# The boundary rows two steps behind VectorE's part, and all three quarters scaled by ScalarE, in a graph network's gather loop

## The reference

```python
h = jnp.maximum(_layernorm(x, axis=-1), 0.0)
# layer 0: attention over the edges, 4 heads, 8 relations
feat_all = jnp.einsum('ni,rhid->rnhd', inputs, conv_weights)
e = jax.nn.leaky_relu(el + er, negative_slope=LEAKY_SLOPE)
ex = jnp.exp(e - m[edge_dst])                     # m: maximum over a destination's edges
alpha = ex / denom[edge_dst]
h = jax.ops.segment_sum(alpha[..., None] * feat_src_e, edge_dst, num_segments=N_NODES)
x = x + h + h_bias
h = jnp.maximum(_layernorm(x, axis=-1), 0.0)
# layer 1: three rounds of mean aggregation, of which the loop prepares the first
h = h @ W_in + b_in
agg = segment_sum(h[src], dst) / deg;  h = relu(agg @ W_agg[l] + h @ W_self[l] + b_hid[l])
```

## Time and profile before

| | us |
|---|---|
| median of 3 runs (2577.82 to 2600.36) | 2599.94 |
| profiled execution, its time | 2594.63 |
| profiled execution, its span | 2592.7 |
| edge loop: first scores (L1393) to last carried row (L1293) | 637.9 to 1461.7 |
| from there to the first load of the next phase | 65.2 |
| busy in the span: PE, DVE, ACT, POOL | 2173, 1388, 718, 585 |

### The profile page before, as it was taken

How to read it: one execution, slowest core, us unless ns; L and a number is a source line. 1 busy time by engine, 2 the same in 40 slices (tenths; PEclk the granted TensorE clock), 3 DMA queues, 4 the chain that set the end, 5 groups by cost and what they waited for, 6 DMA issues and landing times. The chain is left out here.

```text
span 2592.7 us, 29932 instructions
## 1 busy us (share of the span) xinstructions
PE 2173.1 (84%) x9258; PEld 1197.8 (46%) x9259; DVE 1387.6 (54%) x3828; ACT 718.1 (28%) x2133; POOL 584.9 (23%) x549
## 2 busy tenths in 40 slices
PE   2389999995777786778776749999989999999999
PEld 1243334333555464556554424444544444544445
DVE  5779999994456564555565528878821111101001
ACT  0134444442445453445444521010000001000000
POOL 3200000004776665757575100000000000000000
PEclk7589999997776787877777879999989999999999
DMA  5024444445444443535353323222222222233432
GB/s 148 15 97 147 154 148 154 157 154 173 125 126 129 124 140 99 150 103 156 109 152 109 69 89 102 92 82 82 71 83 90 82 86 87 82 115 98 124 98 81
DMA packets 249540, 290.31 MB, mean 112 GB/s; under 512 B 53330, under 2 KB 212247, under 8 KB 249111
## 3 DMA queue, kind: packets, MB, share of 16 engines
q1 hardware_dynamic: 195278, 181.12, 22.8%
q0 software_dynamic: 24192, 67.12, 9.9%
q10 hardware_dynamic: 29896, 39.99, 4.4%
HBM read 201.20 MB, written 86.96 MB: 111 GB/s over the span
## 5 line engine op out<-in xcount | busy, mean ns | idle before, releaser
L1905 PE MATMUL PS<-a_sb,y_sb 128*128 128x512 f16 (+2 forms) x4320 | 874.3, 363 | 43.5 <-DVE y_sb L1981 30.9
L1070 POOL DMA_INDIRECT work<-feat_tab,fidx_i x504 | 543.9, 1079 | 791.3 <-issue 653.1
L1905 PEld LDWEIGHTS PS<-a_sb,y_sb 128*128 128x128 bf16 (+1 forms) x4320 | 407.9, 98 | 509.7 <-issue 69.7
L1275 PE MATMUL PS<-work,stg 128*128 128x260 f32 x1008 | 328.4, 483 | 3.2 <-issue 2.4
L1130 ACT ACTIVATE work<-work 128x64 f32<-128x64 f32 x1344 | 327.3, 332 | 7.5 <-issue 7.1
L233 DVE TENSOR_SCALAR side<-iota_c,col_t 128x512 f16<-128x512 f16 x940 | 329.0, 350 | 0.2
L243 PE MATMUL PS<-side 128*128 128x512 f16 x940 | 254.2, 383 | 20.2 <-DVE side L233 12.4
L1275 PEld LDWEIGHTS PS<-work,stg 128*128 128x128 f32 x1008 | 231.7, 242 | 71.1 <-issue 24.6
L1995 DVE TENSOR_TENSOR mean<-PS,rdeg 128x1024 f32<-128x1024 f32 (+1 forms) x24 | 27.2, 1134 | 416.0 <-PE PS L1905 415.7
L1847 ACT ACTIVATE hT<-mean,bh_c 128x512 f32<-128x512 f32 (+1 forms) x48 | 30.3, 678 | 789.4 <-DVE mean L1999 789.4
L232 DVE TENSOR_SCALAR side<-iota_c,rel 128x128 f16<-128x128 f16 x940 | 236.4, 251 | 0.2 <-PE PS L243 0.2
(11 more groups left out here) (243 smaller groups left out, 1637.0 us busy)
## 6 DMA issues: line engine op xcount, KB each, us to landing
a_sb<-a_tab SPq DMA_DIRECT2D x126, 640.0 KB, 4.3
feat_tab<-stg ACTq DMA_DIRECT2D x120, 260.0 KB, 2.1
a_tab<-side SPq DMA_DIRECT2D x235, 128.0 KB, 1.7
stg<-dst_tab SPq DMA_DIRECT2D x42, 384.0 KB
work<-feat_tab,fidx_i POOLq DMA_INDIRECT x504
h_tab<-outs SPq DMA_DIRECT2D x42, 130.0 KB
h_tab<-outs SPq DMA_DIRECT2D x8, 520.0 KB, 3.2
stg<-h_tab SPq DMA_DIRECT2D x8, 520.0 KB
```

The lines of the kernel that those rows point to most:

```text
L1070: pool.indirect_dma_start(out=ring[:, s, 0:FE], out_offset=None, in_=feat_tab[:, :], in_offset=bass.IndirectOffsetOnAxis(ap=idx, axis=0)). ...
L1275: mm = pe.matmul(PS[:, OUTS[j], 0:EXT], onehot[:, t, :], ring[:, j * U + t, 0:EXT], start=(t == 0), stop=(t == U - 1), skip_group_check=True)
L1905: mm = pe.matmul(SUMS(ug, n)[:, f, :], y_sb[l % 2][0:rows_of, kb, s, f * P:(f + 1) * P], a_sb[0:rows_of, load % SLOTS, kb % KB, 0:n], star ...
```

## The change

- **Scaling.** ACT scales quarter 0 as well, right behind the exponential and ahead of `keep`; DVE's multiplication goes. PE's quarter 0 waits for ACT in place of DVE.
- **Boundary rows.** DVE's part (`ready`) and ACT's `root` stay where they were. PE's and ACT's rows of a chunk now come two steps later (`rows`, at `s - 3 in CHUNK_END`), for chunks 0 to 5.
- **The last two chunks.** Chunk 7 gets its own two PSUM banks and buffers, and the rows of chunks 6 and 7 are done in turns behind the loop (`tail`).
- The output copy goes to the buffer of the first bias copy, no longer to that of ReLU, so the wait for the previous store moves from `turned` to `inner`. SP's stores follow the new places.

```diff
@@ walk(eng, step, begin, ready, rows, tail)
                     step(s // G, s % G, last=(s == SUBS - 1))
                     if s - 1 in CHUNK_END:
-                        part(CHUNK_END.index(s - 1))
-                part(NC - 1)
-                part(NC)
+                        ready(CHUNK_END.index(s - 1))
+                    if s - 3 in CHUNK_END:
+                        rows(CHUNK_END.index(s - 3))
+                tail()
...
@@ ACT step
-                    for half in range(2):
-                        scale(i, j, 2, half)
+                    scale(i, j, 2)
...
                         act.wait_ge(s_rs, num(i, j, 2, 2))
                         weigh(*nxt)
+                        act.wait_ge(s_ex, num(*nxt, 1, 2))
+                        scale(*nxt, 0)
                     keep(i, j)
                     if not last:
-                        act.wait_ge(s_ex, num(*nxt, 1, 2))
-                        for half in range(2):
-                            scale(*nxt, 1, half)
+                        scale(*nxt, 1)
...
+                def tail():
+                    turned(LATE - 1)
+                    root(LATE)
+                    inner(LATE - 1)
+                    turned(LATE)
+                    outer(LATE - 1)
+                    inner(LATE)
+                    outer(LATE)
@@ PE quarter_sum
-                    if q:
-                        pe.wait_ge(s_sa, num(i, j, NQT - 1, q))
-                    else:
-                        pe.wait_ge(s_sd, num(i, j, 1, 1))
+                    pe.wait_ge(s_sa, num(i, j, NQT, q + 1))
...
+                def tail():
+                    turn(LATE - 1)
+                    inner(LATE - 1)
+                    turn(LATE)
+                    outer(LATE - 1)
+                    inner(LATE)
+                    outer(LATE)
@@ DVE
-                def scale(i, j):
-                    dve.wait_ge(s_ex, num(i, j, 1, 2))
-                    tiles = slice(j * U, j * U + QT)
-                    rows = ring[:, tiles, 0:F].rearrange("p u (h d) -> p u h d", h=H)
-                    dve.tensor_tensor(rows, rows, ring[:, tiles, F:FE].unsqueeze(3).to_broadcast([P, QT, H, D]), ALU.mult
-                                      ).then_inc(s_sd, 1)
...
                         bring(i, j)
-                    if not last:
-                        scale(*nxt)
```

More of the change, by code:

```diff
@@ L1039, in at, with walk @@
             return s // G, s % G
-        def walk(eng, step, part, begin):
+        def walk(eng, step, begin, ready, rows, tail):
             with when(eng, 3):
@@ L1058, in walk @@
                     chunk(eng, c, turn)
-                    part(c)
-                part(NC)
+                    if c < NC - 1:
+                        ready(c)
+                        if c:
+                            rows(c - 1)
+                tail()
         with nc.Block() as block:
@@ L1123, in weigh, with scale @@
                     act.activation(fac[:, 0:H], fac_x[:, 0:H], ACT.Exp).then_inc(s_fx, 1)
[L1125 to L1126 removed]
+                def scale(i, j, q):
+                    for u in range(QT):
                         s = j * U + q * QT + u
@@ L1169, in root, with inner, outer, rows @@
                     act.activation(std[:, 0, :], mv[:, 0, :, 1], ACT.Sqrt, bias=eps_c[:, :]).then_inc(s_sd2, 1)
-                def rest(c):
-                    act.wait_ge(s_wi, c + 1)
+                def inner(d):
+                    bank, to = BANKS[late(d)], k2(kept_in[late(d)])
+                    act.wait_ge(s_wi, d + 1)
+                    if d < LATE:
+                        act.wait_ge(s_st, 16 * d + 16)
                     for f in range(K2):
-                        act.activation(k2(h0)[:, f, :], BOUND[:, f, :], ACT.Identity, bias=bin_c[:, f:f + 1]
-                                       ).then_inc(s_h0, 1)
+                        act.activation(to[:, f, :], bank[:, f, :], ACT.Identity, bias=bin_c[:, f:f + 1]).then_inc(s_h0, 1)
                     for f in range(K2):
-                        act.activation(hT[:, f, c * CW:(c + 1) * CW], BOUND[:, f, :], ACT.Identity,
+                        act.activation(hT[:, f, d * CW:(d + 1) * CW], bank[:, f, :], ACT.Identity,
                                        bias=bin_c[:, f:f + 1]).then_inc(s_h0, 1)
[L1179 to L1189, removed]
+                def outer(d):
+                    act.wait_ge(s_t3, d + 1)
+                    act.activation(kept_in[late(d)].rearrange("p (j n) -> p j n", j=2), BANKS[late(d)], ACT.Copy
+                                   ).then_inc(s_tb, 1)
+                def rows(d):
+                    turned(d)
+                    inner(d)
+                    outer(d)
+                def tail():
[6 more added lines that the diff above has]
+                    outer(LATE)
                 def begin(dynamic):
@@ L1196, in begin @@
                     act.wait_ge(s_ex, 2)
-                    for half in range(2):
-                        scale(0, 0, 1, half)
-                walk(act, step, part, begin)
+                    scale(0, 0, 0)
+                    scale(0, 0, 1)
+                walk(act, step, begin, root, rows, tail)
             @block.tensor
@@ L1336, in _ @@
                 pe.wait_ge(built.evicted, NREAL)
-                walk(pe, step, part, begin)
+                walk(pe, step, begin, lambda c: None, rows, tail)
             @block.vector
@@ L1496, in part @@
                     ln_stats(dve, rows, c, 0, s_bs, s_vr)
-                    wait_past(dve, s_t2, c)
-                    ln_finish(dve, rows, c, 0, s_sd2, s_rs2, s_hn, hn)
+                    if c < LATE:
+                        wait_past(dve, s_t2, c)
+                    ln_finish(dve, rows, c, 0, s_sd2, s_rs2, s_hn, hn[late(c)])
                     dve.wait_ge(s_hn, 4 * c + 4)
@@ L1514, in begin @@
                     onehots(0, 0, 1)
-                    scale(0, 0)
-                walk(dve, step, part, begin)
+                walk(dve, step, begin, ready, lambda d: None, lambda: ready(LATE))
             @block.sync
```

82 lines of the change are left out of this document (44 added, 38 removed).

## The result

| | before | after |
|---|---|---|
| median of 4 runs each, us | 2599.06 | 2665.88 |
| ratio, 95% interval | | 1.028 (1.022 to 1.034) |
| profiled execution, span | 2592.7 | 2666.8 |
| first gather to first score | 28.4 | 53.0 |
| first to last score of the loop | 802.1 | 864.9 |

The change makes the kernel 67 us slower; the forecast was 2608, no difference that can be told. A second profile of each kernel gave 30.6, 796.3 (before) and 52.4, 853.9 (after) for the middle two rows.

The account below looks back on a forecast made before the run. The prediction took the chain between PE, DVE and ACT, not gathers, to bound the loop. Scaling +6, boundary +25 and behind the loop -18 gave +13 on 2594.6: 2608 us, 8 in 10 from 2565 to 2650.

Parts of the forecast that it names:

- Scaling, +6: Edge loop steps: moving quarter 0's scaling from DVE to ACT adds 6 us in sum, bounds -34 to +49.
- steps of 18 us have room for it: Plain loop steps: the common 18.0 us step absorbs ACT's added scaling, since its chain needs at least 15.3 us.
- its sign: Profile after, plain stretches of the loop: 18.0 to 18.5 us a step expected.
- seven short steps at 2.4 us: Loop steps under 15 us: each takes at least 2.4 us more through ACT's longer chain, 17 us for seven.
- The ring is full and gathers do not pace the loop: Edge loop: POOL's gathers wait for PE's quarter sums, 110.8 us; the chain between PE, DVE and ACT paces it.
- Boundary, +25: Chunk boundaries in the loop: DVE's parts and rows done apart cost 92 us instead of 67, bounds -8 to +59.
- DVE's part alone: Chunk boundary in the loop: DVE's part without rows costs 3.9 us each, 23 us for six.
- Rows alone: Chunk boundary in the loop: rows without DVE's part cost 11.5 us each, 69 for six, bounds 8.5 and 15.
- Behind the loop, -18: After the loop: last two chunks in turns bring the next phase's load 18 us earlier, bounds -14 to -23.
- ACT becomes the bound: Plain loop steps: PE's late answers add to ACT's longer chain, 20 us a step, 2664 us; chance 0.28 above 2626.
- The ring absorbs the parted boundaries: POOL's waits at loop boundaries: shorter disturbances cost nothing, total 2530 us, or 2565 with half; chance 0.2 below 2574.
- The last sentence of the prediction: Loop: forecast is wrong altogether if PE's lateness, cause unnamed, depends on what DVE or ACT do then; no size given.

Follow-up runs that it names:

- s1_spare: Kernel before, with ACT doing 16 more scalings a step into a spare tile nobody reads, between exponential and keep; ratio 1.012 against before.
- e1_scale: Kernel before with the scaling edit alone: ACT scales quarter 0, DVE no longer does; ratio 1.0235 against before.
- e2_rows: Changed kernel with DVE scaling quarter 0 again; later boundary rows and last two chunks in turns stay; ratio 1.011 against before.
- e3_tail: Kernel before with the last two chunks in turns behind the loop as the one edit; ratio 0.9924, repeated 0.9953, against before.
- p3_pause_all: Changed kernel with two added POOL waits a step, second and third quarter's gathers each waiting for the quarter before to land; 2630.4 us, one run.

## Why the prediction was wrong, by its steps

- **Scaling, +6 (bounds -34 to +49): measured +61 (46 to 76; +49 by medians), at the upper bound or beyond. This is the step that failed.** The sentence "steps of 18 us have room for it" took ACT's idle time for slack. Ahead of the first boundary a plain step did stay at 18.15 us, as its sign asked; between the boundaries it became 19.9 and 20.1. And PE waits for ACT's scaling in most steps, not only in short ones (quarter 0 starts 1.73 us behind the start of `turn_scores` in the median, 0.19 before), so counting seven short steps at 2.4 us missed the others. (From score to score the trace of before has eight steps under 15 us, not seven; nothing hangs on it.) s1_spare shows that a delay on ACT costs though ACT was idle more than half of the time, and in e1_scale POOL's wait for the quarter sums grew. How much of it is the late quarter 0 is open. Where within the 42 steps the 61 us lie the single profiles don't tell: the traces of e1_scale and of before differ by 21 us from first gather to last score (851.1 against 830.4) and 7 behind it, and e1_scale's profiled run was its lowest. Engine time alone (3.9 against 1.2 us a quarter) would have given +113, nearly twice what came; the direction was right.
- **POOL.** "The ring is full and gathers do not pace the loop" was half of it. They don't by their own time, but with a full ring a late quarter sum is a pause of POOL (110.8 us before, 213.6 after), and PE's increments reach DVE late while POOL's run is unbroken. The prediction saw both (PE's late answers, POOL's waits ending when PE resumes) and treated the first as fixed, the second as an effect.
- **Boundary, +25 (-8 to +59): 41 to 49 us, inside the bounds, too small.** Counted as the term is, with the gain behind the loop apart, it is some 6 us more (46.4 against 52.5 us behind the last carried row). DVE's part alone costs 7.0 us over two plain steps in the changed kernel, 6.3 in e2_rows, not 3.9, and above the 6 of its bound: the wait ahead of the reciprocal is 6.5 us, not 3 to 4. Rows alone cost 13.5, not 11.5. Together that is 20.5 us where a joint pair cost 13.2.
- **Behind the loop, -18 (-14 to -23): right.** From last carried row to load 21.3 us less in the first profiles, 20.1 in the second, 18.8 in e2_rows. (The sum lets PE turn chunk 6 at 1467.1, when DVE's last instruction on it starts; it ends 1.2 us later.) e3_tail's 12 to 20 us are another gain, since it still has three chunks behind the loop.
- **Rivals.** "ACT becomes the bound" gave 2664, and 2666 came. Its mechanism is there in part: plain steps of 20 us with PE's quarter 0 behind ACT's scaling stand between the boundaries, but the six ahead of the first boundary stay near 18 (18.5 and 18.3 us, 18.5 and 17.8 before). It had +62 for the scaling, and e1_scale gave +49 to +61; it had +25 for the boundaries, and they cost more, so that the total fits so closely is luck. "The ring absorbs the parted boundaries" doesn't happen here; it nearly does in p3_pause_all, where POOL paces the steps. The last sentence of the prediction, that PE's lateness might depend on others, named the right doubt and the wrong engines: by p3_pause_all it depends on POOL.

The Trainium skill has a sentence that would have warned, in "Perfetto Trace Analysis", Per-instruction lifecycle, Tensor Engine Instruction: the end of a matmul's record is estimated, and the semaphore's way behind it lies outside the record. The trace agrees: an end at 761.2, an increment at 766.9.

## What to carry to other kernels

Where a group of waits says "remote", compare the time at which the awaited work's record ends with what other engines do until the wait ends; here 16 of 20 long ones ended 2.3 to 3.5 us after POOL's last gather began. Idle time of an engine is no slack if its result gates the refill of a full ring: cost such an edit by who waits for the ring's release, not by the engine's busy share. And a wait that looks like loss can be gain: one more wait of POOL in each step took 51 us off the changed kernel.

## What the runs showed of the hardware

- PE's semaphore increments come up to 10 us after their records' ends in the loop (1279.5 to 1289.7), 27 us at the start (633.0 to 659.6), while POOL issues indirect gathers one each 1.25 us, several then within 0.2 us. They are not always held: of the 42 of `turn_scores` in the changed kernel 17 come within 0.2 us. Two pauses in a step of twelve gathers, 2.6 and 2.7 us in the median, nearly remove it (p3_pause_all, one profile); one pause doesn't.
- What in the chip holds them (the issuing of the gathers, or their transfers) is open: a pause waits for both.
